# Cross-attention in a decoder layer: denominators summed by DMAs that add into SBUF, straight code, and a sixth rounded product

## The reference, cut to what matters

```python
q = (hidden_states @ Wq).reshape(B, Sq, H, D)          # H = 16 heads of D = 128
k = (encoder_hidden_states @ Wk).reshape(B, Skv, H, D) # Skv = 1500 context rows of 128 channels
v = (encoder_hidden_states @ Wv).reshape(B, Skv, H, D)
q = rmsnorm(q, gq)
k = rmsnorm(k, gk)
scores = jnp.einsum('bqhd,bkhd->bhqk', q, k) * scale
attn = jax.nn.softmax(scores, axis=-1)
out = jnp.einsum('bhqk,bkhd->bqhd', attn, v)
out = out.reshape(B, Sq, H * D)
return out @ Wo
```

## Time and profile before

| | us |
|---|---|
| three runs, median | 1362.12 |
| three runs, lowest and highest | 1360.58, 1363.41 |
| the profiled execution, its own time | 1365.66 |
| the profiled execution, span from first to last instruction | 1363.8 |

### The profile page before, as it was taken

One profiled execution on the slowest core, in us unless ns is written; L12 is line 12 of the kernel. 1 busy time (PEld: TensorE's weight loads), 2 busy tenths in 40 slices (PEclk: granted clock), 3 DMA queues, 4 the chain that ended last, 5 costly groups with the idle time before them and its releaser, 6 DMA issues. The chain is left out here.

```text
span 1363.8 us, 25118 instructions
## 1 busy us (share of the span) xinstructions
PE 1321.3 (97%) x6366; PEld 1041.6 (76%) x6366; DVE 1104.1 (81%) x1742; ACT 1026.5 (75%) x3157; POOL 1040.8 (76%) x926
## 2 busy tenths in 40 slices
PE   8889899999999999999999999999999999999878
PEld 4667578777777777777777777777777777778667
DVE  5766589888888888888888888888888888875275
ACT  2557688888888888888888888888888888843342
POOL 3733212898989898989898989898989898998840
PEclk9799999999999999999999999999999999999979
DMA  7040000101010101010100000000000010010200
GB/s 246 32 166 1 25 1 9 38 12 35 13 35 13 36 12 34 12 35 12 34 15 32 16 30 19 29 20 26 24 23 27 19 31 16 18 68 25 71 0 28
DMA packets 28012, 45.59 MB, mean 33 GB/s; under 512 B 2720, under 2 KB 23840, under 8 KB 27120
## 3 DMA queue, kind: packets, MB, share of 16 engines
q1 hardware_dynamic: 27168, 44.25, 9.9%
q10 hardware_dynamic: 720, 0.10, 0.0%
HBM read 40.41 MB, written 3.93 MB: 33 GB/s over the span
## 5 line engine op out<-in xcount | busy, mean ns | idle before, releaser
L1302 PE MATMUL xa_k_ps<-wk_parts,xa_ctxT_hi 128*125 128x512 f32 x768 | 377.1, 491 | 6.1 <-DVE wk_parts L1295 5.0
L1245 DVE TENSOR_REDUCE xa_ss<-xa_sq 125x6 f32<-125x768 f32 x360 | 339.4, 943 | 1.0 <-ACT xa_sq L1183 1.0
L1233 DVE TENSOR_TENSOR xa_scores<-xa_s_ps,xa_rk 125x448 f32<-125x448 f32 x384 | 238.5, 621 | 99.8 <-PE xa_s_ps L1304 98.0
L1303 PE MATMUL xa_k_ps<-wk_parts,xa_ctxT_hi 128*125 128x512 f32 x768 | 304.1, 396 | 0.0
L1304 PE MATMUL xa_k_ps<-wk_parts,ctxT_lo 128*125 128x512 f32 x768 | 303.1, 395 | 0.0
L1095 POOL TENSOR_TENSOR xa_den<-probs,xa_den 125x896 f32<-125x896 f32 x128 | 272.2, 2126 | 0.0
L1168 ACT ACTIVATE probs<-xa_scores 125x896 f32<-125x896 f32 x192 | 183.6, 956 | 105.2 <-POOL xa_scores L1084 39.3
L1148 ACT ACTIVATE xa_sq<-xa_k_ps 125x512 f32<-125x512 f32 x360 | 212.2, 589 | 42.3 <-PE xa_k_ps L1304 21.8
L1182 ACT ACTIVATE xa_k_ps<-xa_k_ps 125x128 f32<-125x128 f32 x720 | 189.2, 263 | 30.7 <-PE xa_k_ps L1304 28.6
L1387 PE MATMUL xa_o_ps<-probs,xa_ctx_nat 125*128 125x448 f32 x448 | 205.4, 539 | 0.0
L1084 POOL TENSOR_TENSOR xa_scores<-xa_scores,xa_gmax 125x896 f32<-125x896 f32 x96 | 203.9, 2124 | 0.1
(11 more groups left out here) (186 smaller groups left out, 2364.7 us busy)
## 6 DMA issues: line engine op xcount, KB each, us to landing
xa_ctx_nat<-in_ctx SPq DMA_DIRECT2D x16, 750.0 KB
ctxT_in<-in_ctxT SPq DMA_DIRECT2D x84, 125.0 KB, 2.1
qo<-in_xq_w SPq DMA_DIRECT2D x1, 2048.0 KB, 11.0
qo<-in_xo_w SPq DMA_DIRECT2D x1, 2048.0 KB, 19.0
vo_scratch<-qo SPq DMA_DIRECT2D x2, 1024.0 KB, 5.0
vo<-vo_scratch SPq DMA_DIRECT2D x1, 2048.0 KB, 9.2
ctxT_in<-in_ctxT SPq DMA_DIRECT2D x2, 750.0 KB, 8.9
xq_wkT<-in_xk_wT SPq DMA_DIRECT2D x4, 256.0 KB, 4.3
```

The lines of the kernel that those rows point to most:

```text
L1233: dve.tensor_tensor(scores[0:KP, j, :, :], raw, key_scale, ALU.mult).then_inc(s_taken, 1)
L1245: dve.tensor_reduce(ss[:, i // 2, UH * (i % 2):UH * (i % 2) + vector_heads(of)], squares(of, i).rearrange("p (g d) -> p g d", d=XD), AX.X, ...
L1302: pe.matmul(out, l_hi, r_hi, start=first, stop=False)
L1303: pe.matmul(out, l_hi, r_lo, start=False, stop=False)
```

## The change

- Each of the last four pairs of a half (y % 12 = 4, 6, 8, 10) is added to `den2` by a DMA that GpSimd issues, with addition into the destination in SBUF. The add of the first two pairs stays a GpSimd instruction. Each DMA waits until the one before it has landed (`den_landed`), and so does whatever used to wait for an add: the fold, the low parts of probabilities, ScalarE before it overwrites a slot of the ring.
- Tile 1 is split too: six of twelve weighted sums in a half are three rounded products (SPLIT_PAIRS, ODD_PARTS, and the conditions in ScalarE, GpSimd and TensorE).
- The fold comes one step later, the low part of the probabilities one step later (so that it now stands behind the add or DMA of the next pair), the weighted sum one step later.
- All phases are straight code.

```diff
-def each_phase(eng, body, loop_end):
-    for b in (-1, 0, 1):
-        body(Phase(b))
-    with eng.Fori(1, loop_end // 2) as pair:
-        for i in range(2):
-            body(Phase(None, pair, i))
-    for b in range(loop_end, B + 1):
+def each_phase(body):
+    for b in range(-1, B + 1):
         body(Phase(b))
...
-FOLD_LAG = DEN_LAG + 1
-ADDS = KT // 2
-PV_LAG = EXP_LAG + 5
-LOW_LAG = EXP_LAG + 3
+FOLD_LAG = DEN_LAG + 2
+ACCUMULATIONS = KT // 2 - 2
+PV_LAG = EXP_LAG + 6
+LOW_LAG = EXP_LAG + 4
...
-def adds_done(ph, y):
-    half, k = y // KT, y % KT // 2
-    return ph.at(2 * ADDS, ADDS * half + max(k, 1))
+def wait_added(eng, den_done, den_landed, ph, y):
+    if y % KT < 4:
+        wait(eng, den_done, ph.at(4, 2 * (y // KT) + 1))
+    else:
+        wait(eng, den_landed, ph.at(32 * ACCUMULATIONS, 16 * (ACCUMULATIONS * (y // KT) + y % KT // 2 - 1)))
...
-SPLIT_PAIRS = KT // 2 - 1
+SPLIT_PAIRS = KT // 2
...
-ODD_PARTS = ((1, 3), (3, 6))
+ODD_PARTS = ((0, 3), (3, 6))
...
                         if y % KT == 2:
-                            wait(pool, den_done, ph.at(2 * ADDS, ADDS * (y // KT)))
-                            so_far = probs_pair(y - 2)
+                            wait(pool, den_done, ph.at(4, 2 * (y // KT)))
+                            pool.tensor_tensor(den2[:, :, :], probs_pair(y), probs_pair(y - 2), ALU.add
+                                               ).then_inc(den_done, 1)
                         else:
-                            wait(pool, den_done, ph.at(2 * ADDS, ADDS * (y // KT) + y % KT // 2 - 1))
-                            so_far = den2[:, :, :]
-                        pool.tensor_tensor(den2[:, :, :], probs_pair(y), so_far, ALU.add).then_inc(den_done, 1)
+                            wait_added(pool, den_done, den_landed, ph, y - 2)
+                            pool.dma_start(den2[:, :, :], probs_pair(y), accum_op=ALU.add).then_inc(den_landed, 16)
...
-                        wait(pool, den_done, ph.at(2 * ADDS, ADDS * (y // KT + 1) - 1))
+                        wait_added(pool, den_done, den_landed, ph, y)
                         pool.tensor_tensor(den[:, :], den2[:, 0, :], den2[:, 1, :], ALU.add).then_inc(den_done, 1)
                     y = lagged_pair(ph, j, LOW_LAG)
-                    if y is not None and y % KT:
+                    if y is not None:
                         pool.wait_ge(p_hi_ready, pairs_split(ph, y))
-                        pool.wait_ge(den_done, adds_done(ph, y))
+                        wait_added(pool, den_done, den_landed, ph, y)
...
-                        if y % KT:
-                            act.activation(p_hi[:, y // 2 % (NPR // 2), :], score_slot(y + 1), ACT.Exp
-                                           ).then_inc(p_hi_ready, 1)
+                        act.activation(p_hi[:, y // 2 % (NPR // 2), :], score_slot(y + 1), ACT.Exp
+                                       ).then_inc(p_hi_ready, 1)
...
-                        if ty % 2 and ty > 1:
+                        if ty % 2:
```

More of the change, by code:

```diff
@@ L836, in lagged_pair @@
     return y if y is not None and y % 2 == 0 else None
-def adds_done(ph, y):
-    half, k = y // KT, y % KT // 2
-    return ph.at(2 * ADDS, ADDS * half + max(k, 1))
+def wait_added(eng, den_done, den_landed, ph, y):
[3 more added lines that the diff above has]
+        wait(eng, den_landed, ph.at(32 * ACCUMULATIONS, 16 * (ACCUMULATIONS * (y // KT) + y % KT // 2 - 1)))
 def vector_shifts(y):
     return y % KT < KT // 2
-SPLIT_PAIRS = KT // 2 - 1
+SPLIT_PAIRS = KT // 2
 def pairs_split(ph, y):
-    return ph.at(2 * SPLIT_PAIRS, SPLIT_PAIRS * (y // KT) + y % KT // 2)
-ODD_PARTS = ((1, 3), (3, 6))
+    return ph.at(2 * SPLIT_PAIRS, SPLIT_PAIRS * (y // KT) + y % KT // 2 + 1)
+ODD_PARTS = ((0, 3), (3, 6))
 def early_products(ph, j):
@@ L949, in odd_hi @@
             first, last = ODD_PARTS[part]
-            return nat_hi[:, ph.parity(), first - 1:last - 1, :]
+            return nat_hi[:, ph.parity(), first:last, :]
         def probs_pair(y):
@@ L979, in cross_attention @@
         max_turned, qmax_ready, max_spread = sem("xa_max_turned"), sem("xa_qmax_ready"), sem("xa_max_spread")
+        den_landed = sem("xa_den_landed")
         shift_done, exp_done, den_done, pv_done = (
@@ L1028, in _ @@
             sp.dma_start(ident_in, a.ident).then_inc(ident_loaded, 16)
-            each_phase(sp, body, 12)
+            each_phase(body)
         @block.gpsimd
@@ L1116, in body @@
                         q_low(ph.shift(h), 1 - h)
-            each_phase(pool, body, 14)
+            each_phase(body)
         @block.scalar
@@ L1166, in body @@
                         if ph.b is None or STEPS * ph.b + y >= NPR:
-                            wait(act, den_done, adds_done(ph, y - NPR))
+                            wait_added(act, den_done, den_landed, ph, y - NPR)
                         act.activation(probs_pair(y), score_pair(y), ACT.Exp).then_inc(exp_done, 2)
-                        if y % KT:
-                            act.activation(p_hi[:, y // 2 % (NPR // 2), :], score_slot(y + 1), ACT.Exp
-                                           ).then_inc(p_hi_ready, 1)
+                        act.activation(p_hi[:, y // 2 % (NPR // 2), :], score_slot(y + 1), ACT.Exp
+                                       ).then_inc(p_hi_ready, 1)
                     if j in NAT_SPLITS and ph.within(0, 15):
@@ L1185, in body @@
                     if splits_den(ph, j):
-                        act.wait_ge(den_done, ph.at(2 * ADDS, ADDS * (h - 1)))
+                        act.wait_ge(den_done, ph.at(4, 2 * (h - 1)))
                         act.activation(den_hi[:, :], den[:, :], ACT.Copy).then_inc(den_hi_ready, 1)
@@ L1214, in _ @@
             q_high(Phase(0), 0)
-            each_phase(act, body, 14)
+            each_phase(body)
         @block.vector
@@ L1296, in _ @@
                                   ).then_inc(wk_lo_ready, 1)
-            each_phase(dve, body, 14)
+            each_phase(body)
         @block.tensor
@@ L1353, in body @@
                         if ph.b == B:
-                            pe.wait_ge(den_done, ph.at(2 * ADDS, ADDS * (h - 1)))
+                            pe.wait_ge(den_done, ph.at(4, 2 * (h - 1)))
                             pe.matmul(out, ones[:, 0:1].broadcast_to([KP, P]), den[:, :],
@@ L1379, in body @@
                                 pe.wait_ge(nat_lo_ready, of.at(2, 2))
-                        if ty % 2 and ty > 1:
+                        if ty % 2:
                             pe.wait_ge(p_lo_ready, pairs_split(ph, y - 1))
-                            three(o_ps[:, hy, 0:UW], nat_hi[:, of.parity(), ty // 2 - 1, :],
+                            three(o_ps[:, hy, 0:UW], nat_hi[:, of.parity(), ty // 2, :],
                                   nat_r[:, of.parity(), ty, :], p_hi[:, (y - 1) // 2 % (NPR // 2), :],
@@ L1398, in _ @@
             pe.wait_ge(ones_r_set, 1)
-            each_phase(pe, body, 14)
+            each_phase(body)
 def output_and_mlp(nc, a, qo, hT_hi, hT_lo, vo, late, early_ps):
```

## The result

The changed kernel takes **1482.57 us**, the median of four runs (1478.99 to 1485.56), against 1362.76 for the kernel before on the same chip. The ratio is 1.0883, with a 95% interval of 1.0862 to 1.0903: 8.8% slower. The forecast was 1358.2, in a range that ended at 1375. It had the wrong sign, and the range didn't hold the result.

A forecast was written before the change was run, and what follows sets the result against it. TensorE was taken to bound the middle and GpSimd's chain the end. Terms of -4.3, -1.6 and +2.0 summed to -3.9 us, from the median 1362.12 to 1358.2 us, range 1354 to 1375 for 8 times in 10.

The forecast's parts named there:

- L: Round trip of an adding DMA from issue to landing, taken as 3.8 us, between 3.1 and 4.4.
- The decision point: Round trip, L, of 5.9 us, from which GpSimd's chain overruns a half of 33.5 us.
- Rival 1: Landings overrun the half, DMAs held to about five engines, L 5.4 to 9.1: about 1370 to 1510 us, chance 0.25.
- The fixed part: GpSimd's serial work in a half besides four round trips: 9.9 us, in 9.9 + 4L.
- the sixth product: One more rounded product per half on TensorE: 0.14 us each, 31 times, -4.3 us; extra ScalarE and GpSimd work hidden.
- The adds that become DMAs: nothing in the middle: 128 adds leave GpSimd, 17 us a phase; no gain in the middle, since GpSimd was not the bound there.
- The last half: -1.6 us for the chain: Chain at the end: +0.3 us up to the fold's end, -1.9 us from there to the next block.
- The term for the start: Last half's chain starts later, as two earlier DMAs meet the late loads: 0 to +4.0 us, taken as +2.0.
- The term for the fold's new place: At the end, denominators' sum goes ahead of the last weighted sum: fold's end to next block 6.3 to 4.4 us, -1.9.
- Straight code: nothing: All phases as straight code change nothing; phase 1 and phase 3 differ by 0.01 us.
- GpSimd's busy time: Over the whole kernel, to fall by about 235 us (272 - 37).
- Rivals 2 and 3: The first: end gives it back, 1362 us, chance 0.31; the second: L 3.1, no sharing, 1354.8 us, within faster 0.44.

## Why the prediction was wrong

**The failing step: L.** "I take 3.8, between them", from loads of 125 and 1024 KB, with bounds of 3.1 and 4.4. It measured 6.0 us. The copy fits the guess: 3.9 us. What failed is the bound for the addition, "If the addition makes it read twice, the line gives 4.4 us for 896 KB". A DMA that adds isn't a copy of twice the bytes; between 218.8 and 437.5 KB it runs at about 100 GB/s (an estimate from two landings). The line drawn through plain loads could not contain that, and nothing in the profile before showed an adding DMA. The upper bound should not have been taken from that line alone.

**The decision point was right in form and generous in size.** Rival 1 said that from L = 5.9 the half overruns. At a landing of 6.0 that would be 9.9 + 24 = 33.9 us, 0.4 too much; measured were 36.6. The fixed part is 10.56, not 9.9, because the low part of the first pair, which the sixth product adds, stands in it: 1.1 us, less a pause of 0.49 us that the kernel before had in the same place. The prediction counted that low part as hidden in GpSimd's spare time. And the trip from one issue to the next is 6.4 to 6.6 us (6.0 to 6.2 to the fold), as GpSimd, idle by then, starts its next DMA some 0.5 us after the landing. With these, the point is (33.5 - 10.6) / 4 = 5.7 us from issue to issue.

**Rival 1 happened, by another mechanism.** It had the DMA held to about five engines. It isn't. Busy time by stretch while one of them moves, in the changed kernel:

```profile
732.00:733.00 1.00, 1.00 (x6) 0.82 (x6) 0.72 (x1) 1.00 (x7) 1.00 (x3) 1.00 1.04 108
733.00:734.00 1.00, 1.00 (x8) 0.86 (x7) 0.68 (x2) 0.74 (x2) 1.00 (x1) 1.00 0.86 86
```

The share is 1.04 of 16 engines at 108 GB/s, where late loads move 414 at 1.01. All engines are taken, and each is slow. The Trainium skill ("DMA: Bandwidth & Descriptors", on why a DMA increments its semaphore by 16) says that some copies issued from GpSimd use all 16 engines, also where 16 doesn't divide the partitions. The share of 1.04 agrees with it, for a DMA that adds. The Trainium skill, same page, gives in the anatomy of one DMA 2.0 us plus bytes at 436 GB/s, an estimate of 3.0 us for this one. The copy took 3.9 and the addition 6.0, and the measurement decides.

**"The adds that become DMAs: nothing in the middle" had a second hole.** I shared the DMA engines only with the late loads and `vo`, not with the context load in 125-partition rows that comes in each phase. It costs 13 us in the changed kernel (1482.57 to 1469.55 with the load cut in two) and as much with half the columns (1383.75 to 1371.01). At L = 3.9 the middle of the copies' kernel still loses up to 2 us a phase by it. The forecast would have been too low even with the right L for a copy.

**The end was priced once instead of four times.** "The last half: -1.6 us for the chain" prices one half. GpSimd has little room in all of phases 15 and 16: the earlier trace rows has it at 55.9 of 61.4 and 30.3 of 30.9 us, and I took the second row alone. (TensorE is as full there, but early output products fill it in.) The four halves there cost 39 us, of which adds on GpSimd give 26.6 back. The term for the start, +2.0 from two DMAs that share the engines with the late loads, came as one trip of 10.2 us, 3.7 over the usual 6.5. And the load of `vo`, which TensorE was to cover, stands beside a trip of 8.4 us in the half that loses most, 14 us.

**The term for the fold's new place** was -1.9 us from the fold to the next block, and 0.8 came. The sum of the denominators did move ahead of the last weighted sum, but it takes 1.83 us, where the earlier trace rows has 0.91. In order of time, TensorE in the changed kernel:

```profile
1411.61 1.83 PE L1352 MATMUL xa_s_ps<-xa_den,xa_ones 125*128 125x448 f32 x2 [2.66 <-POOL xa_den L1100]
1412.60 1.21 PE L1299 MATMUL xa_o_ps<-xa_p_hi,xa_nat_hi 125*128 125x448 f32 x1
...
1416.93 3.32 PE L1581 MATMUL om_ps<-vo,qo 128*128 128x256 f32 x7 [2.37 <-PEq L890]
```

The clock explains it. Busy time by stretch in the changed kernel, ahead of the closing and in it:

```profile
1396.00:1411.60 15.60, 8.21 (x26) 4.84 (x25) 0.00 (x0) 0.84 (x2) 5.25 (x6) 0.83 0.49 61
1411.60:1417.00 5.40, 3.02 (x6) 1.53 (x6) 1.95 (x4) 1.21 (x3) 0.95 (x1) 0.50 0.00 0
```

The granted clock is 0.50 in the closing, the lower of the two levels, 1.2 GHz; TensorE had been busy 8.2 of the 15.6 us before it. From the start of that sum to the next block it is 5.32 us here, and 4.41 in the kernel before and in the three kernels with the adds put back, where the sum itself takes 0.91 or 0.92 us. In the first of them, with only the adds put back, the term is -1.4 (7.39 to 5.99 us). In the one with early shifts it is +0.2, since there TensorE is itself late: the fold ends at 1285.36, and its sum starts at 1287.41.

**The sixth product** was right in size and wrong in cover. "9.8 us is a wide margin" compared busy times over a phase. The order on GpSimd's queue decided: a shift came behind its due time, 0.56 us of TensorE a phase. And with four halves at the end in which GpSimd has hardly a pause, what 14 phases gain is lost again there. "Straight code: nothing" holds for the phases.

**GpSimd's busy time** was to fall by about 235 us and fell by 115. The sum left out the 128 issues, which the page counts with 107 us (their rows overlap the next ones in part), and the low parts take 72 us more, not 37.

**Rivals 2 and 3** needed an L of 3.1 to 4.4, and no run with additions of full width had one. The chance of 0.25 for rival 1 was too low, since the range of L was borrowed from plain loads alone.

**Left open.** Why the addition is slow (the read of the destination, the size of its pieces, or the adding itself) wasn't tried; nor whether DMAs that add side by side, into separate buffers, would land sooner; nor what the one-step-later fold, low part and weighted sum cost by themselves.

## What to carry to other kernels

A price that no row shows should be bounded by what would break the plan, not by the rows nearest to it: here the plan stood only below 5.7 us a trip, and one DMA that adds, measured alone, would have settled it. Work moved from an engine to a chain of dependent DMAs isn't free because the engine has less to do; each trip stands in the queue of the engine that issues and waits. And where an engine sets the pace in some stretch, count every instruction added to it there: the sixth low part took back in four halves what it had gained in twenty-eight, until VectorE took seven additions from it.

## What the runs showed of the hardware

- A DMA from GpSimd within SBUF, 125 partitions x 896 f32 (437.5 KB): 3.9 us to land as a copy, 6.0 with an addition; half the columns with an addition, 3.8.
- The row of its issue on GpSimd is 0.54 us long as a copy and 0.84 with an addition (0.89 with half the columns), but the next instruction starts 0.54 and 0.57 us behind it: an addition holds the queue hardly longer.
- Likewise GpSimd's first low part behind the issue of an adding DMA ends later (1.39 to 1.48 us instead of 1.16; behind a copy's issue 1.16), while the next instruction starts 1.1 us behind it, as ever: the difference is in when it ends, not in what it costs the queue.
- The adding DMA fills 16 engines at 86 to 108 GB/s, and a load that meets it is slowed as well: the 125 KB loads land in 3.6 us instead of 2.1.
- A load in rows of 125 partitions that meets such a DMA delays it, 8.5 us to the next issue instead of 4.4 to 5.0 (half the columns); cut into 112 and 13 partitions it leaves every phase at 67.01 to 67.08 us.
- How much it delays depends on when the DMA is issued: with all columns, 4.2 us behind the load 7.2 to 8.3 us to the next issue, 2.4 to 2.9 us behind it 9.0 to 10.0, and 6.5 to 6.6 with the load cut in two.
